# The split of the row maxima into two bf16 parts, moved from VectorE to the head of GpSimd's step

## What is computed

```python
q = _apply_rotary(q_emb, split_heads(_proj(x, Wq, bq)))
k = _apply_rotary(k_emb, split_heads(_proj(c, Wk, bk)))
scores = jnp.einsum('bhtc,bhsc->bhts', q, k) / math.sqrt(K_CH)
p_attn = jax.nn.softmax(scores, axis=-1)
out = jnp.einsum('bhts,bhsc->bhtc', p_attn, v)
```

## Time and profile before

| | |
|---|---|
| median of three runs | 881.02 us (879.29 to 883.98) |
| the profiled execution | 880.23 us |
| its span, first to last instruction | 878.4 us |
| mean granted TensorE clock | 0.945 |
| TensorE, VectorE, ScalarE, GpSimd busy | 85%, 71%, 58%, 51% of the span |

### The profile page before, as it was taken

One profiled execution on the slowest core, in us unless ns is written; L12 is line 12 of the kernel. 1 busy time (PEld: TensorE's weight loads), 2 busy tenths in 40 slices (PEclk: granted clock), 3 DMA queues, 4 the chain that ended last, 5 costly groups with the idle time before them and its releaser, 6 DMA issues. The chain is left out here.

```text
span 878.4 us, 23052 instructions
## 1 busy us (share of the span) xinstructions
PE 743.0 (85%) x6138; PEld 530.9 (60%) x6139; DVE 627.2 (71%) x1653; ACT 512.1 (58%) x1213; POOL 450.4 (51%) x929
## 2 busy tenths in 40 slices
PE   3699999999999999999999999962899299999900
PEld 2356666766766666666666666531566188888700
DVE  6877898898899888888888899638333134444467
ACT  3155777777777777777777777651555045555400
POOL 5444555645645555555564563122777535656510
PEclk9999999999999999999999999985799799999965
DMA  8597344444444444444434469720222345555379
GB/s 255 137 301 220 107 125 122 105 128 124 109 120 113 125 114 118 123 106 129 121 105 127 123 177 287 237 68 1 97 106 106 124 117 153 145 155 156 98 227 347
DMA packets 112404, 126.46 MB, mean 144 GB/s; under 512 B 14189, under 2 KB 98928, under 8 KB 112369
## 3 DMA queue, kind: packets, MB, share of 16 engines
q1 hardware_dynamic: 105456, 109.11, 45.0%
q0 software_dynamic: 6912, 16.93, 5.2%
HBM read 76.93 MB, written 50.63 MB: 145 GB/s over the span
## 5 line engine op out<-in xcount | busy, mean ns | idle before, releaser
L797 DVE TENSOR_REDUCE M<-bank_s 128x2 f32<-128x512 f32 x512 | 339.7, 685 | 60.6 <-PE bank_s L1050 55.3
L600 ACT ACTIVATE Pr<-bank_st 128x512 f32<-128x512 f32 x512 | 295.6, 598 | 122.9 <-PE bank_st L1078 117.8
L1050 PE MATMUL bank_s<-QK 72*128 72x256 bf16 x1024 | 201.4, 280 | 13.1 <-DMA QK<-parts 11.1
L1078 PE MATMUL bank_st<-QK 98*128 98x256 bf16 x1024 | 197.8, 275 | 1.3 <-ACT Pr L600 1.1
L1033 PE MATMUL bank_o<-Pr,wide 128*32 128x256 f32 x2048 | 139.5, 388 | 0.0
L1050 PEld LDWEIGHTS bank_s<-QK 72*128 72x128 bf16 x1024 | 93.3, 102 | 70.7 <-DVE M L797 34.3
L525 POOL TENSOR_TENSOR work<-work 128x256 f32<-128x256 f32 x64 | 46.8, 731 | 162.6 <-DVE work L855 162.6
L940 DVE TENSOR_TENSOR OT<-work,bank_st 128x128 f32<-128x128 f32 x112 | 32.2, 288 | 136.2 <-ACT work L681 136.2
L1078 PEld LDWEIGHTS bank_st<-QK 98*128 98x128 bf16 x1024 | 97.8, 98 | 27.4 <-ACT Pr L600 4.6
L571 POOL DMA_INDIRECT results<-QK,ids_out x80 | 78.4, 980 | 64.9 <-issue 49.4
L1184 PE MATMUL bank_st<-wgu,xT_sb 128*128 x320 | 84.4, 387 | 0.0
(11 more groups left out here) (145 smaller groups left out, 1218.5 us busy)
## 6 DMA issues: line engine op xcount, KB each, us to landing
QK<-parts SPq DMA_DIRECT2D x128, 288.0 KB
parts<-parts_sb SPq DMA_DIRECT2D x128, 96.0 KB, 2.3
slots<-xT_sb SPq DMA_DIRECT2D x8, 1300.0 KB, 6.3
wide<-slots SPq DMA_DIRECT2D x80, 130.0 KB, 2.3
ctx_kv<-ctx_dram SPq DMA_DIRECT2D x64, 128.0 KB, 2.1
QK<-results SPq DMA_DIRECT2D x16, 512.0 KB, 8.2
X<-x_dram SPq DMA_DIRECT2D x8, 512.0 KB, 7.8
parts<-parts_sb SPq DMA_DIRECT2D x64, 64.0 KB, 2.1
```

Source lines behind the costliest of these rows:

```text
L600: nc.scalar.activation(Pr[k][:], bank_st[k % 2][:], ACT.Exp, scale=SCALE).then_inc(s_exp, 1)
L797: nc.vector.tensor_reduce(M[:, c, 2 * k:2 * k + 2], bank_s[S_BANK[c][k]][:].rearrange("p (a s) -> p a s", a=2), AX.X, ALU.max).then_inc(s_ ...
L1050: last = nc.tensor.matmul(bank_s[S_BANK[at.mod(2)][k]][:, T * t:T * t + T], Q[c][0:KR, k, P * t:P * t + P], K[c][0:KR, k, :], start=True, ...
L1078: last = nc.tensor.matmul(bank_st[k % 2][:, T * s:T * s + T], K[c][0:MROW + 2, k, P * s:P * s + P], Q[c][0:MROW + 2, k, :], start=True, st ...
```

## The change

Both instructions of the split leave VectorE's step, where they stood behind the first reduce (k = 0), and go to GpSimd's, as its first work, ahead of Newton and the rotary sum. The waits and the signals are the same ones. The copy that rounded to bf16 is now a subtraction of zero: `newton[:, 2:3]` holds 0.0 and is broadcast over the 16 columns.

```diff
--- before.py
+++ after.py
@@ -499,6 +499,16 @@
             pool.wait_ge(s_blank, 2)
 
             def step(at):
+                if at.has(1):
+                    c = at.mod(2, 1)
+
+                    wait(pool, s_red, at.value(8, 16))
+                    wait(pool, s_TM, at.value(1, 0))
+                    nc.gpsimd.tensor_tensor(Mb[:, c, 0, :], M[:, c, :], newton[:, 2:3].to_broadcast([P, 2 * H]),
+                                            ALU.subtract).then_inc(s_hi, 1)
+                    wait(pool, s_hi, at.value(1, 2))
+                    nc.gpsimd.tensor_tensor(Mb[:, c, 1, :], M[:, c, :], Mb[:, c, 0, :],
+                                            ALU.subtract).then_inc(s_msp, 1)
                 if at.r % 2 == 0 and at.has(-4):
 
                     p = at.odd_pair(-4)
@@ -797,15 +807,6 @@
                         nc.vector.tensor_reduce(M[:, c, 2 * k:2 * k + 2],
                                                 bank_s[S_BANK[c][k]][:].rearrange("p (a s) -> p a s", a=2),
                                                 AX.X, ALU.max).then_inc(s_red, 1)
-                    if k == 0 and at.has(1):
-                        c = at.mod(2, 1)
-
-                        wait(dve, s_red, at.value(8, 16))
-                        wait(dve, s_TM, at.value(1, 0))
-                        nc.vector.tensor_copy(Mb[:, c, 0, :], M[:, c, :]).then_inc(s_hi, 1)
-                        wait(dve, s_hi, at.value(1, 2))
-                        nc.vector.tensor_tensor(Mb[:, c, 1, :], M[:, c, :], Mb[:, c, 0, :],
-                                                ALU.subtract).then_inc(s_msp, 1)
                     if k == 2 and at.r % 2 == 1 and at.has(-3):
                         pair = at.pair(-3)
                         xp = X[:, bass.ds(pair, 1), :].rearrange("p a t -> p (a t)")
```

## The result

| | before | after |
|---|---|---|
| median of 20 runs | 880.97 us | 888.90 us |
| ratio, with its 95% interval | | 1.0092 (1.0075 to 1.011) |
| the profiled execution, and its span | 880.23, 878.4 us | 888.25, 886.5 us |
| mean granted TensorE clock | 0.945 | 0.938 |

The account below looks back on a forecast made before the run. The prediction took TensorE to bound the loop: 880.2 us for the profiled execution, plus 8.6 for late odd transposes over 26 pairs and 1.1 at the start, gives 889.9, stated as 890, range 883 to 897.

Parts of the forecast that it names:

- TensorE sets the pace: In the loop, TensorE is the bound and VectorE waits for it; a pair of steps takes 16.79 us.
- Part 1: Two split instructions leave VectorE, 17.0 and 19.9 us in 64 executions each; the return was costed at nothing.
- TensorE covers it: VectorE's reduces wait for back-to-back TensorE work, so freed VectorE time, up to 36.9 us, returns nothing.
- Part 2: Two 128x16 instructions added to GpSimd, each 0.22 us long and 0.30 apart; the broadcast zero costs nothing.
- S: Time from the end of GpSimd's last rotary instruction, through the split, to TensorE's transpose: 0.61 us.
- Part 3: Waits at the transposes: 8.61 even to odd, 8.51 odd to even; 0.33 us more a pair, +8.6 over 26.
- The seed's 0.79: In an even step, GpSimd's Newton chain starts 0.79 us after TensorE reaches the transpose.
- The start: At the program's start, the first transpose waits behind GpSimd's work and goes at 39.67, 1.08 later: +1.1 us.
- The upper end of the range: With a split delay of 0.75 us, a pair takes 8.75 + 8.63 = 17.38; +15.3 us with the start, 896.6.
- dear form: Rival: each GpSimd split instruction costs as one of 128x256; a pair is 18.90, in all 936 us; chance 0.04.
- hidden after all: Rival: TensorE's 0.60 us idle a pair before L1101 absorbs late odd transposes; 881.3 us; chance 0.12.
- VectorE was the bound: Rival: TensorE's weight-load waits for VectorE are real, so relieving VectorE gives about 854 us; chance 0.06.

Follow-up runs that it names:

- e7: The kernel before, with ScalarE's copy for the router put ahead of the first exponential of its step; ratio to before 0.9756, 16.14 us a pair.
- e8: The change with the split ahead of GpSimd's last rotary instruction, and ScalarE's router copy put first; ratio to the kernel before 0.9734, 15.99 us a pair.
- e3: The change, with the split moved ahead of the previous step's last rotary instruction on GpSimd; ratio to the kernel before 0.9949, 16.72 us a pair.
- e1: The change, with two Newton rounds in place of three; ratio to the kernel before 0.996, 16.72 us a pair.
- e2: The kernel before, with two Newton rounds in place of three; ratio to before 0.9941, 16.72 us a pair.
- e6: The kernel before, with one more VectorE instruction in each step, behind the split; ratio to before 1.006, 17.06 us a pair.
- e5: The change again, unaltered, on a second, slower chip; ratio to the kernel before there 1.0109, 17.11 us a pair.
- e4: The change, with two more dependent 128x16 GpSimd instructions ahead of the split; ratio to the kernel before 1.0221, 17.56 us a pair.

## Why the prediction was right, point by point

- **TensorE sets the pace:** right. e7 shows it from the other side: 0.60 us of its idle time taken away give 0.65 a pair, and 0.73 where the split is early (e8 against e3).
- **Part 1, VectorE's return worth nothing:** right in the sum (e1 and e2 are the same to a hundredth of a us a pair). The amount was too high: the page's busy time of VectorE fell by 28.4 us, not 36.9; neighbouring rows of an engine overlap by some 0.08, as the row after L807 does. GpSimd's rose by 23.5 and not 28, for the same reason. "TensorE covers it" was too broad. e6 shows that 0.34 us more in the odd step comes through, by way of L814's bank.
- **Part 2, S = 0.61:** measured 0.60. The 128x16 instructions take 0.22 us (forecast 0.22), 0.29 apart (0.30). The broadcast operand costs nothing that shows.
- **Part 3, the pair:** forecast 8.61 and 8.51, measured 8.59 to 8.62 and 8.50 to 8.51. The seed's 0.79 is 306.85 - 306.05 = 0.80. Even transposes don't wait, as forecast. The 26 pairs gave 7.7 us and not 8.6: a steady pair grew by 0.31 and not 0.33, which is 0.5 of it, and the first and the last pair grew by less than the steady ones, which is 0.4.
- **The start, +1.1:** wrong. The step "the first transpose goes at 39.67, 1.08 later" took the start of GpSimd's work from the one profile. The waits are there (1.28 and 0.66 us), but this start had its rotary part over at 37.54, not 39.06. The first of the 26 pairs began 0.3 us later than before, which is all that came of the 1.1, and in e1, e2, e3, e5 and e6 it begins anywhere from 98.1 to 101.2. One execution can't price a term of 1 us there. The measured time lies in the range with this term or without it.
- **The sum:** 889.9 for the profiled execution, which took 888.25; the two misses, 0.9 and 0.8, went the same way. The median is 888.9, and the 20 executions lie between 883.3 and 894.5.
- **The upper end of the range:** mis-sized. For S = 0.75 the prediction adds the even transpose's wait to the pair, 8.75 + 8.63 = 17.38. e4 shows that this wait runs beside the way to the seed: 8.51 + 8.00 + 0.75 = 17.26, some 893.5 in place of 896.6. The dear form's 936 has the same mistake; 8.51 + 8.00 + 1.51 = 18.02 gives some 913. The forecast of 890 doesn't rest on it, since at S = 0.61 even transposes don't wait.
- **The rivals:** "hidden after all" falls by the result and by e4, in both of which the 0.60 us before the router's logits are still there, "VectorE was the bound" by e1 and e2, the dear form by the 0.22 us. What the Trainium skill says in Perfetto Trace Analysis, "Optimizing Scalar/DVE Operations", of work moved from VectorE to GpSimd came out by its cautious half (it might not help), but not for its reason, the shared port: e3 keeps both instructions on GpSimd and loses nothing. VectorE was busy for 88% of the stretch from 200 to 500 us before, and for 92% in e7, where its split is the late one. The rule of SBUF — State Buffer, "Who interferes with whom", agrees with e7's stretched L807: 0.65 us, to 0.03 behind the end of GpSimd's L534, where the unstretched one takes 0.17. It can't be told from these runs which of the port's conditions each instruction met.

## What to carry to other kernels

Before moving work to an engine with idle time, look at when that engine is idle, not at how much: GpSimd was half idle, but not in the 0.4 us before the transpose, and one place further up its queue the same move costs nothing. Write the loop as the later of several ways to the same event, each from its own starting point; when one event waits, the ways that start ahead of it don't move. And an engine's room matters only at the places where somebody waits for it, so test it there.

## What was not expected of the hardware

- On two of the three chips the kernel before took 57 to 59 us more; the change in e5 took 58.0 more (946.9 against 888.9), all of it behind the attention. In e5's profile, while GpSimd scatters the rows (until about 701 us), ScalarE stands idle up to 14.1 us before single instructions, with only "remote" in the profile as what ended it, and TensorE up to 21.7 us, with only "issue". The granted clock of TensorE is 0.54 from 660 to 700 us, where TensorE is busy for 6.9 us; in the first run of the change it was 0.97, with 30.9 us busy. What causes it wasn't tried.
- On GpSimd the spacing of small instructions depends on their waits: in e4 the second extra one, which waits for the first, starts 0.29 after it (315.10 + 0.51 - 0.22 = 315.39), and the split's first, which waits for nothing new, 0.17 after that (315.56).
